# Edge counting in 29 spans of unequal widths, formed one span ahead

## The chip, the cores and the metric

One Trainium2 chip, one core of it. The metric is the device time of one execution in microseconds; lower is better. The core's engines work in parallel, each on its own list of instructions: PE (TensorE) multiplies matrices into PSUM, DVE (VectorE) and ACT (ScalarE) do elementwise work, POOL (GpSimd) gathers rows, SP (SyncE) starts transfers. They wait for one another by semaphores.

## What is computed

A graph transformer of two layers on 1250 nodes with 768 features and 20,000 edges `(src, dst)`, sorted by `dst`. The first layer adds an edge attention (12 heads), a linear attention without softmax (`mix`) and a mixture of experts; the second a graph convolution, another mixer and another mixture of experts. What matters here is the part of the first layer that needs the edges:

```
dst = minimum(int(1250 * uniform(20000) ** 2), 9999);  order = argsort(dst)
xn  = layernorm(x)
e   = leaky_relu(a1[src] + a2[dst]);  w = exp(e - segment_max(e, dst)[dst])
agg = segment_sum(w / denom[dst] * ft[src], dst)       # the edge attention
q, k, v = elu(xn @ w_qkv) + 1 ...;  out = (q (k^T v)) / (q sum(k)) @ w_proj
x   = x + relu(agg + res) + out
```

Edges are not evenly spread: `dst` is the square of a uniform number, so the number of edges that end below node n is about 20000 * sqrt(n / 1250). The first 50 nodes receive some 4,000 edges, the last 50 some 400.

## The kernel before

**Counting.** The kernel turns the edge list into a dense matrix `AT[s, d]`, the number of edges from s to d, and does the attention on it. It counts by matmuls of one-hot rows. The edges lie in 160 tiles of 125 edges. A node `src` is written as (row `src mod 125`, block `src div 125`). For a span of `WD` = 50 destination nodes, DVE forms for each tile that holds edges of the span two one-hot matrices: `OHS` (125 edges x 128 rows, from `io128`) and `OHK` (125 edges x 500 columns, from `iok`, column = 10 * (dst - first node) + block). PE multiplies the two and accumulates in a PSUM bank: 125 x 500 counts. ACT copies the bank into `AT` (`counts_out`). There are `NW` = 25 spans of 50 nodes.

**Turns.** A span's tiles are worked in turns of `SLOTS` = 3 tiles, in a hardware loop on DVE (`hot_rows`) and one on PE (`span_counted`). How many turns a span has is worked out on the chip from the edges (a table that both engines load) and is at least 2. The formed matrices go through a ring of `RING` = 4 turns, so DVE can be at most four turns ahead of PE. The counts alternate between two PSUM banks (`WB` = 2), which leaves six banks for the other work.

**Where the counting stands.** Spans 0 to 12 (`QSPANS`, `WQ` = 13) are counted between the 18 rounds in which PE computes the queries of the linear attention (L830, six q blocks times three column chunks): after rounds 1 to 13 PE counts one span each. In each round ACT takes an exponential of the result (L1243, L1245), DVE combines it into `QT` (L1756). DVE forms span r - 1 ahead of its emptying of round r. I call this the query stage. Spans 13 to 24 are counted in the tile stage, ten node tiles t of 125 nodes: for each PE transposes the attention rows of tile t (L856), makes the rows of tile t + 2 (`linear`, L847), counts the first span of `TILE_SPANS[t]`, multiplies by the projection for tile t - 1 in two halves (L864), with the tile's second span, if any, between the halves. DVE does in tile t: `normal_rows(t + 2)` (L1764, L1768), the forming of the tile's second span, the addition of one projection half (`add_half`, L1776), the forming of the *first* span of tile t + 1, and the other addition. Before `linear(0)`, PE waits until DVE has emptied all 18 query rounds. SP loads the projection's weights once 13 spans have left PSUM.

Behind the tile stage comes the edge attention proper, which needs the whole of `AT`; then the mixtures of experts and the second layer, which don't depend on the counting otherwise.

With the inputs of this case the turns of the 25 spans are 11, 5, 4, 3, 3, 3, 3, 3 and then 2 each: 45 in the query stage and 24 in the tile stage, 69 in all.

Of the kernel before, what the change touches and what calls it, by code (L numbers as in the profile page):

```python
# [32 lines left out]
CH = [(0, 418), (418, 416), (834, 416)]  # L33
# [20 lines left out]
WSLOTS = 6  # L54
QSPANS = {r: r - 1 for r in range(1, 14)}
WQ = len(QSPANS)
TILE_SPANS = [[WQ + t + (t > 3) + (t > 6)] + ([WQ + t + (t > 3) + 1] if t in (3, 6) else []) for t in range(NT)]
assert [w for t in TILE_SPANS for w in t] == list(range(WQ, NW))
FILLS = [(p, t0, nt) for p in range(NP) for t0, nt in ((0, 4), (4, 4), (8, 2))]
FILL_AT = {1: 0, 4: 1, 6: 2}  # L60
DEN_AT = {3: (1, 3), 7: (5, 7), 9: (9,)}
# [99 lines left out]
def graph_transformer(nc, xn_d, y_d, x, src, dst, gW, gWT, gWresT, attnT, w0, wp0, bp0, rwT, rb, ewT, eb,  # L161
                      W1, b1c, W2, b2, w1, wp1, bp1, fgT, fbg, fW1, fb1, fW2, fb2, out):
    J = plan_jobs()


    cursor = [(nc.sbuf_base + 63) // 32 * 32]
# [118 lines left out]
    vv = sb("vv", [P, 2 * H])  # L285
    iok = sb("iok", [T, KW], F16)
    gidx = sb("gidx", [80, 2, NW])
    gidx_i = sb("gidx_i", [80, 2, NW], I32)
    tidx = sb("tidx", [80, 2])
    tidx_i = sb("tidx_i", [80, 2], I32)  # L290
    mnx = sb("mnx", [80, 2, 2])
    hit = sb("hit", [80, 2, 2, NW])
    rng = sb("rng", [2 * NW, 1])
    span = sb("span", [1, 8, NW])
    table = sb("table", [1, 3, NW], I32)
    assert cursor[0] <= top - XNB * C * 4 - 8192
# [288 lines left out]
    def _(pool):  # L585
# [6 lines left out]
        nc.gpsimd.iota(k128_i, pattern=[[P, 32]], base=0, channel_multiplier=0).then_inc(consts, 1)  # L592
        nc.gpsimd.iota(tq_i, pattern=[[1, NT]], base=0, channel_multiplier=0).then_inc(consts, 1)
        nc.gpsimd.iota(io128_i, pattern=[[1, P]], base=0, channel_multiplier=0).then_inc(consts, 1)
        nc.gpsimd.iota(gidx_i, pattern=[[WD, 2], [WD, NW]], base=0, channel_multiplier=0).then_inc(consts, 1)
        nc.gpsimd.iota(tidx_i, pattern=[[80, 2]], base=0, channel_multiplier=1).then_inc(consts, 1)
        nc.gpsimd.iota(iok_i, pattern=[[1, KW]], base=0, channel_multiplier=0).then_inc(consts, 1)

# [96 lines left out]
    def _(pe):  # L695
# [104 lines left out]
            emptied(J.last_in(8 - WB + b, J.at["q0_0"]))  # L800

        def span_counted(w):
            ps = PS[:, 8 - WB + w % WB, 0:KW]
            OHS, OHK = (OHSA, OHKA) if w < WQ else (OHSB, OHKB)

            def counted(first):
                formed = nc.tensor.snap(formed_r, min_val=0, max_val=2 * SLOTS * TURNS * NW)
                ring = nc.tensor.snap(ring_r, min_val=0, max_val=RING - 1)
                for k in range(SLOTS):
                    pe.wait_ge(oh_ready, formed + 2 * k + 2)  # L810
                    nc.tensor.matmul(ps, OHS[:, bass.ds(ring, 1), k, :].rearrange("p a c -> p (a c)"),  # L811
                                     OHK[:, bass.ds(ring, 1), k, :].rearrange("p a c -> p (a c)"),
                                     start=(first and k == 0), stop=True, skip_group_check=True).then_inc(oh_free, 1)
                nc.tensor.reg_alu(formed_r, formed_r, 2 * SLOTS, ALU.add)
                nc.tensor.reg_alu(ring_r, ring_r, 1, ALU.add)
                nc.tensor.reg_alu(ring_r, ring_r, RING - 1, ALU.bitwise_and)

            if w >= WB:
                pe.wait_ge(at_ready, w - WB + 1)
            counted(True)  # L820
            with nc.tensor.Fori(1, turns_of[w]):
                counted(False)
            nc.tensor.matmul(ps[:, 0:16], zeros, zeros[:, 0:16], start=False, stop=True,
                             skip_group_check=True).then_inc(acc_done, 1)

        for q in range(KC):
# [8 lines left out]
            if q == 1:  # L835
# [2 lines left out]
                for k in range(NT):  # L838
                    last = nc.tensor.transpose(ps[0:T, k * H:(k + 1) * H], ARW[0:H, k * T:(k + 1) * T], ident[0:H, 0:H])
                last.then_inc(pe_filled, 1)  # L840
        pe.wait_ge(dve_emptied, J.emptied("dve", J.at[f"q0_{KC - 1}"] + 2))

        def linear(t):
            for b in range(2):
                ps = begin(J.at[f"lin{t}"] + b)
                for p in range(3):
                    last = nc.tensor.matmul(ps[0:T, p * (P + 2):(p + 1) * (P + 2)], QT[:, 3 * b + p, t * T:(t + 1) * T],  # L847
                                            KVB[:, 3 * b + p, :], start=True, stop=True)
                last.then_inc(pe_filled, 1)
# [377 lines left out]
    def _(act):  # L1227
# [38 lines left out]
        def counts_out(w):  # L1266

            act.wait_ge(acc_done, w + 1)
            nc.scalar.activation(AT[:, :, w * WD:(w + 1) * WD], PS[0:T, 8 - WB + w % WB, 0:KW].rearrange("p (d s) -> p s d", s=NT),
                                 ACT.Copy).then_inc(at_ready, 1)  # L1270

        for r in range(18):
# [251 lines left out]
    def _(dve):  # L1524
# [75 lines left out]
        for t in range(NT):  # L1600
# [126 lines left out]
        def hot_rows(w):  # L1727

            OHS, OHK = (OHSA, OHKA) if w < WQ else (OHSB, OHKB)
            nc.vector.reg_alu(tile_r, window[w], TBITS - 1, ALU.bitwise_and)  # L1730
            nc.vector.reg_alu(end_r, window[w], (1 << 20) - TBITS, ALU.bitwise_and)
            with nc.vector.Fori(0, nc.vector.snap(end_r, min_val=2 * TBITS, max_val=TURNS * TBITS), TBITS):
                done = nc.vector.snap(done_r, min_val=0, max_val=SLOTS * TURNS * NW)
                ring = nc.vector.snap(ring_r, min_val=0, max_val=RING - 1)
                tile = nc.s_assert_within(nc.vector.snap(tile_r, min_val=0, max_val=TBITS - 1), 0, ETP - SLOTS,
                                          skip_runtime_bounds_check_because=
                                          "a window's first tile is at most ETP less the tiles of its turns")
                for k in range(SLOTS):
                    dve.wait_ge(oh_free, done + k + 1)
                    V.tensor_scalar(OHS[:, bass.ds(ring, 1), k, :].rearrange("p a c -> p (a c)"), io128,  # L1740
                                    ES[:, 0, bass.ds(tile + k, 1)], None, ALU.is_equal).then_inc(oh_ready, 1)
                    V.tensor_scalar(OHK[:, bass.ds(ring, 1), k, :].rearrange("p a c -> p (a c)"), iok,
                                    ES[:, 1, bass.ds(tile + k, 1)], -float(KW * w), ALU.subtract,
                                    ALU.is_equal).then_inc(oh_ready, 1)
                nc.vector.reg_alu(tile_r, tile_r, SLOTS, ALU.add)
                nc.vector.reg_alu(done_r, done_r, SLOTS, ALU.add)
                nc.vector.reg_alu(ring_r, ring_r, 1, ALU.add)
                nc.vector.reg_alu(ring_r, ring_r, RING - 1, ALU.bitwise_and)

        for r in range(18):  # L1750
            o, n = CH[r % 3]
            if r in QSPANS:
                hot_rows(QSPANS[r])
            ps = full(J.at[f"q0_{r // 3}"] + r % 3)
            dve.wait_ge(qexp, r + 1)
            V.scalar_tensor_tensor(out=QT[:, r // 3, o:o + n], in0=ps[:, 0:n], scalar=0.0, in1=TQ[r % 4 // 2][:, r % 2, 0:n],  # L1756
                                   op0=ALU.max, op1=ALU.add).then_inc(dve_emptied, 1)
# [446 lines left out]
```

## Time and profile before

| | us |
|---|---|
| time, median of 3 runs | 1899.55 (1899.08 to 1900.85) |
| profiled execution, its own time | 1895.67 |
| its span in the profile | 1893.9 |
| mean granted TensorE clock, share of full | 0.969 |
| PE busy | 1774.6 (94%) |
| DVE busy | 723.1 (38%) |
| ACT busy | 391.8 (21%) |

The span runs from the first to the last instruction of the profiled execution; a few microseconds of its time lie around it. Engines overlap, so the busy times don't add up to the span. "PEld" is PE's loading of the stationary operand, which lies beside its multiplying; "PEldq" and "DVEq" rows are an engine's sequencer at work on registers and branches. In a timeline each row is a start, a length, an engine, a line of the kernel, an operation with output and input, and a count of merged instructions; in brackets stands the idle time of the engine before it and who released it.

### The profile page before, as it was taken

What the parts mean: (1) busy time and instruction counts of PE and PEld (TensorE: products, weight loads), DVE (VectorE), ACT (ScalarE), POOL (GpSimd) and SP (SyncE); (2) the same over time, 40 slices, a digit from 0 to 9 for tenths busy, and PEclk for the clock granted to TensorE, in tenths of its full rate; (3) what the DMA queues carried; (4) which work ended last, traced back from release to release, by engine and by line L of the source; (5) the groups of instructions that cost most, each with busy time, mean ns of one, the idle gap of its engine ahead of it and who ended that gap; (6) DMA issues with size and microseconds to landing.
All of it is one profiled execution on the core that took longest, in us unless ns stands there. A gap on an engine that the chain in (4) does not pass through costs nothing.

```text
span 1893.9 us, 24577 instructions
## 1 busy us (share of the span) xinstructions
PE 1774.6 (94%) x7984; PEld 1088.4 (57%) x7985; DVE 723.1 (38%) x1799; ACT 391.8 (21%) x1030; POOL 130.3 (7%) x170
## 2 busy tenths in 40 slices
PE   7999899999999986899997999999999999789996
PEld 4555455664333343566666855555579569656664
DVE  4321674555789897211116211151111114522221
ACT  2441022112422222110113321000221221112221
POOL 0000000000000000111114000000000000012222
PEclk9999799999999998899998999999999999889999
DMA  6002101000001014355636011010010012535773
GB/s 195 1 0 71 57 2 61 1 1 33 26 28 49 28 39 149 134 189 180 211 132 189 29 50 50 0 50 0 0 51 1 0 58 87 219 78 148 203 189 60
DMA packets 53660, 144.38 MB, mean 76 GB/s; under 512 B 9806, under 2 KB 20450, under 8 KB 53125
## 3 DMA queue, kind: packets, MB, share of 16 engines
q1 hardware_dynamic: 34053, 87.05, 13.3%
q0 software_dynamic: 12032, 36.23, 7.9%
q10 hardware_dynamic: 7488, 19.93, 3.0%
q8 instruction: 55, 0.90, 0.2%
q14 instruction: 32, 0.26, 0.0%
HBM read 114.08 MB, written 33.99 MB: 78 GB/s over the span
## 4 chain that ended last, share of the span: by engine, by line
PE 84%; DVE 8%; DMA 2%; issue 2%; DVEq 2%; ACT 1%; ACTq 0%; POOL 0%; SPq 0%; POOLq 0%
PE PS L723 21%; PE PS L1064 10%; PE PS L733 8%; PE PS L1174 5%; PE PS L1196 5%; PE PS L830 4%; PE PS L864 4%; PE PS L1146 4%; PE PS L1132 4%; PE PS L1105 4%; DVE WRA L1849 3%; PE PS L970 3%; PE PS L811 3%; PE PS L1042 2%; PE PS L979 2%
## 5 line engine op out<-in xcount | busy, mean ns | idle before, releaser
L723 PE MATMUL PS<-WS,XT 128*125 128x384 f32 x960 | 312.9, 488 | 1.4 <-issue 1.4
L723 PEld LDWEIGHTS PS<-WS,XT 128*125 128x125 f32 x960 | 180.2, 189 | 129.1 <-issue 3.0
L1064 PE MATMUL PS<-WS,XGT 128*128 x600 | 199.3, 489 | 0.0
L1064 PEld LDWEIGHTS PS<-WS,XGT 128*128 128x128 f32 x600 | 113.0, 192 | 74.4 <-issue 1.9
L733 PE MATMUL PS<-XT,WS 128*128 128x416 f32 (+1 forms) x432 | 151.2, 512 | 0.0
L1849 DVE SCALAR_TENSOR_TENSOR WRA<-RB,U,AT 125x500 f32<-125x500 f32 (+1 forms) x240 | 140.0, 647 | 2.5 <-issue 0.6
L1983 DVE TENSOR_TENSOR YS<-PS,EBB 128x768 f32<-128x768 f32 x48 | 46.0, 958 | 243.9 <-PE PS L1064 191.1
L733 PEld LDWEIGHTS PS<-XT,WS 128*128 128x128 f32 x432 | 81.6, 189 | 69.2 <-issue 69.2
L970 PE MATMUL PS<-WRA,F 125*64 125x500 f32 (+1 forms) x480 | 100.0, 527 | 10.2 <-DVE WRA L1849 9.1
L614 POOL DMA_INDIRECT XG<-xn_rows,IDX x53 | 52.1, 982 | 749.1 <-DVEq L1944 641.7
L1174 PE MATMUL PS<-WS,XGT 128*128 x288 | 99.7, 497 | 1.1 <-ACTq L1393 1.1
L1196 PE MATMUL PS<-WS,HT 128*128 x276 | 92.9, 486 | 1.1 <-DVE YS L1983 1.1
L1391 ACT ACTIVATE XGT<-PS 128x384 f32<-128x384 f32 x102 | 44.5, 488 | 227.4 <-DVE YS L1983 176.2
L830 PE MATMUL PS<-XT,WS 128*128 128x416 f32 (+1 forms) x216 | 83.4, 540 | 0.3 <-DVEq L1714 0.3
L864 PE MATMUL PS<-WS,QT 128*125 128x384 f32 x240 | 80.2, 490 | 0.0
L1105 PE MATMUL PS<-XT,WS 128*128 128x250 f32 x360 | 78.3, 378 | 0.6 <-issue 0.6
L1468 ACT ACTIVATE HF<-PS,DT 125x384 f32<-125x384 f32 x40 | 23.2, 581 | 263.0 <-PE PS L723 263.0
L723 PE MATMUL PS<-WS,QK 128*125 128x384 f32 x240 | 77.6, 486 | 0.0
L2070 DVE TENSOR_TENSOR HH<-HF,HH 125x384 fp32r<-125x384 f32 x40 | 22.3, 558 | 136.5 <-ACT HH L1470 136.5
L1174 PEld LDWEIGHTS PS<-WS,XGT 128*128 128x128 f32 x288 | 54.1, 195 | 34.9 <-issue 4.2
L1196 PEld LDWEIGHTS PS<-WS,HT 128*128 128x128 f32 x276 | 52.4, 190 | 37.6 <-issue 1.3
L1105 PEld LDWEIGHTS PS<-XT,WS 128*128 128x128 f32 x360 | 68.7, 192 | 9.1 <-issue 1.0
(314 smaller groups left out, 2105.0 us busy)
## 6 DMA issues: line engine op xcount, KB each, us to landing
WS<-in_ewT SPq DMA_DIRECT2D x8, 2304.0 KB, 10.6
WS<-in_fW SPq DMA_DIRECT2D x16, 1152.0 KB, 6.9
WS<-in_w SPq DMA_DIRECT2D x5, 2304.0 KB, 10.4
expert_rows<-YS ACTq DMA_DIRECT2D x25, 384.0 KB, 2.3
xn_rows<-XN ACTq DMA_DIRECT2D x20, 336.0 KB
RB<-expert_rows SPq DMA_DIRECT2D x12, 488.3 KB
WS<-in_wp SPq DMA_DIRECT2D x2, 2304.0 KB, 8.4
WS<-in_W SPq DMA_DIRECT2D x2, 2304.0 KB, 8.4
```

Of the source, the lines that this page charges most:

```text
L723: last = nc.tensor.matmul(ps[0:T, 0:HC], lhsT[:, k, t * T:(t + 1) * T], w[:, k, b * HC:(b + 1) * HC], start=(k == 0), stop=(k == KC - 1))
L733: last = nc.tensor.matmul(ps[:, 0:n], w[:, k, q * P:(q + 1) * P], rhs[:, k, o:o + n], start=(k == 0), stop=(k == KC - 1))
L830: last = nc.tensor.matmul(ps[:, 0:n], w[:, k, q * P:(q + 1) * P], XT[:, k, o:o + n], start=(k == 0), stop=(k == KC - 1))
L864: last = nc.tensor.matmul(ps[0:T, 0:HC], QT[:, k, t * T:(t + 1) * T], w[:, k, b * HC:(b + 1) * HC], start=(k == 0), stop=(k == KC - 1))
L970: last = nc.tensor.matmul(num[j * D:(j + 1) * D], F[:, s, 2 * p + j, 0:D], WR[k % WSLOTS][:, j, 0:n], start=(s == 0), stop=(s == NT - 1), ...
L1064: last = nc.tensor.matmul(PS[:, 4 + 2 * a + b, 0:HC], XGT[:, a, k, :], WS[:, bass.ds(slot, 1), k * C + b * HC:k * C + (b + 1) * HC].rearra ...
L1105: last = nc.tensor.matmul(ps[:, 0:n], w[:, k, q * P:(q + 1) * P], XT[:, k, o:o + n], start=(k == 0), stop=(k == KC - 1))
L1132: last = nc.tensor.matmul(ps[:, 0:n], HH[:, v, s, q * P:(q + 1) * P], AT[:, s, o:o + n], start=(s + v == 0), stop=(s == NT - 1 and v == 1))
L1146: last = nc.tensor.matmul(ps[0:T, 0:HC], AT[:, s, t * T:(t + 1) * T], HH[:, v, s, b * HC:(b + 1) * HC], start=(s + v == 0), stop=(s == NT ...
L1174: last = nc.tensor.matmul(PS[:, 2 + a, 0:FH], XGT[:, a, k, :], WS[:, bass.ds(slot, 1), k * FH:(k + 1) * FH].rearrange("p a b -> p (a b)"), ...
L1196: last = nc.tensor.matmul(PS[:, 5 + b, 0:HC], HT[:, k, :], WS[:, bass.ds(slot, 1), o:o + HC].rearrange("p a b -> p (a b)"), start=(k == 0) ...
L1849: V.scalar_tensor_tensor(out=WR[k % WSLOTS][:, j, 0:nt * T], in0=RBS[u % RSLOTS][:, j, 0:nt * T], scalar=U[:, s, h:h + 1], in1=AT[:, s, t0 ...
```

## The change

The destination nodes are cut into 29 spans. 21 are 50 nodes wide and go downward from the last node to node 200 (`START` = 1200, 1150, ... 200); eight more start at 153, 112, 78, 50, 28, 12, 3 and 0, with widths 47, 41, 34, 28, 22, 16, 9 and 3. The compare for `OHK`, the matmul and the copy to `AT` run over the span's own width (`kw` = 10 x width columns) instead of 500. The query stage counts the first 13 spans in the new order (nodes 1200 down to 600), the tile stage the other 16: one, then two in tiles 1 to 6, then one in tiles 7 to 9. DVE forms span 0 ahead of the query rounds, and span r ahead of its emptying of round r, one span earlier than before. PE's wait before `linear` is for the column chunk that tile t needs. The spans' limits, by which the table of turns is made, are written by 16 more small memsets on DVE.

```diff
-NW = N // WD
+WIDE = 21
+NARROW = [153, 112, 78, 50, 28, 12, 3, 0]
+NW = WIDE + len(NARROW)
+START = [N - WD * (w + 1) for w in range(WIDE)] + NARROW
+WIDTH = [WD] * WIDE + [a - b for a, b in zip([START[WIDE - 1]] + NARROW, NARROW)]
...
-TILE_SPANS = [[WQ + t + (t > 3) + (t > 6)] + ([WQ + t + (t > 3) + 1] if t in (3, 6) else []) for t in range(NT)]
+NSPANS = [1, 2, 2, 2, 2, 2, 2, 1, 1, 1]
+TILE_SPANS = [list(range(WQ + sum(NSPANS[:t]), WQ + sum(NSPANS[:t + 1]))) for t in range(NT)]
...
         def span_counted(w):
-            ps = PS[:, 8 - WB + w % WB, 0:KW]
+            kw = WIDTH[w] * NT
+            ps = PS[:, 8 - WB + w % WB, 0:kw]
...
-                                     OHK[:, bass.ds(ring, 1), k, :].rearrange("p a c -> p (a c)"),
+                                     OHK[:, bass.ds(ring, 1), k, 0:kw].rearrange("p a c -> p (a c)"),
...
-        pe.wait_ge(dve_emptied, J.emptied("dve", J.at[f"q0_{KC - 1}"] + 2))
-
         def linear(t):
+            c = next(c for c, (o, n) in enumerate(CH) if (t + 1) * T <= o + n)
+            pe.wait_ge(dve_emptied, J.emptied("dve", J.at[f"q0_{KC - 1}"] + c))
...
         def counts_out(w):
...
-            nc.scalar.activation(AT[:, :, w * WD:(w + 1) * WD], PS[0:T, 8 - WB + w % WB, 0:KW].rearrange("p (d s) -> p s d", s=NT),
+            nc.scalar.activation(AT[:, :, START[w]:START[w] + WIDTH[w]],
+                                 PS[0:T, 8 - WB + w % WB, 0:WIDTH[w] * NT].rearrange("p (d s) -> p s d", s=NT),
...
             if t == 0:
+                for w in range(WIDE, NW):
+                    V.memset(gidx[:, 0, w:w + 1], float(START[w]))
+                    V.memset(gidx[:, 1, w:w + 1], float(START[w] + WIDTH[w]))
                 dve.wait_ge(e_in, 32)
                 V.tensor_copy(EF, EI).then_inc(edge_f, 1)
...
-                    V.tensor_scalar(OHK[:, bass.ds(ring, 1), k, :].rearrange("p a c -> p (a c)"), iok,
-                                    ES[:, 1, bass.ds(tile + k, 1)], -float(KW * w), ALU.subtract,
+                    V.tensor_scalar(OHK[:, bass.ds(ring, 1), k, 0:kw].rearrange("p a c -> p (a c)"), iok[:, 0:kw],
+                                    ES[:, 1, bass.ds(tile + k, 1)], -float(NT * START[w]), ALU.subtract,
                                     ALU.is_equal).then_inc(oh_ready, 1)
...
+        hot_rows(0)
         for r in range(18):
             o, n = CH[r % 3]
-            if r in QSPANS:
-                hot_rows(QSPANS[r])
+            if r in QSPANS and QSPANS[r] + 1 < WQ:
+                hot_rows(QSPANS[r] + 1)
```

The first place is DVE at the start of the query stage. `OHSA` and `OHKA` are the one-hot buffers of the spans of this stage, `QT<-PS,TQ` is the emptying of a query round, `L1732` and `L1745` the loop over a span's turns. Before, around the emptyings of rounds 0 and 1:

```order
L1721 MEMSET zeros 125x64
L1756 SCALAR_TENSOR_TENSOR QT<-PS,TQ_104 128x418
...
L1740 TENSOR_SCALAR OHSA<-io_66,ES 125x128
L1742 ISA
L1742 TENSOR_SCALAR OHKA<-iok,ES 125x500
...
L1732 COMPARE_AND_BRANCH
L1756 SCALAR_TENSOR_TENSOR QT<-PS,TQ_104 128x416
```

And in the changed kernel:

```order
L1733 MEMSET zeros 125x64
...
L1753 TENSOR_SCALAR OHSA<-io_66,ES 125x128
L1755 ISA
L1755 TENSOR_SCALAR OHKA<-iok,ES 125x500
...
L1745 COMPARE_AND_BRANCH
L1770 SCALAR_TENSOR_TENSOR QT<-PS,TQ_104 128x418
...
L1745 COMPARE_AND_BRANCH
L1770 SCALAR_TENSOR_TENSOR QT<-PS,TQ_104 128x416
```

A loop of forming now stands ahead of the emptying of round 0 as well; the emptying of round 1 has the loop of span 1 ahead of it and no longer that of span 0.

The second place is PE in the tile stage, from the first projection half of one tile to the counting of the next; `OHKB` and `OHSB` are the one-hot buffers of this stage, `L823` and `L831` close a span. Before, at a tile with one span:

```order
L823 MATMUL PS<-zeros 128x16
L864 MATMUL PS<-WS,QT 125x384 x12
L856 MATMUL PS<-ident,LO 128x125 x6
L847 MATMUL PS<-KVB,QT 125x130 x6
...
L811 MATMUL PS<-OHKB,OHSB 128x500
```

In the changed kernel, at the end of tile 4 and the start of tile 5:

```order
L872 MATMUL PS<-WS,QT 125x384 x6
...
L819 MATMUL PS<-OHKB,OHSB 128x470
...
L831 MATMUL PS<-zeros 128x16
L872 MATMUL PS<-WS,QT 125x384 x6
L864 MATMUL PS<-ident,LO 128x125 x6
L855 MATMUL PS<-KVB,QT 125x130 x6
...
L819 MATMUL PS<-OHKB,OHSB 128x410
```

The projection of a tile, 12 matmuls in a row before, is now cut in two by a span in tiles 1 to 6, and the counting matmuls have the span's own width.

## Rows read from the trace of the kernel before

**Rows 1.** Chain of work that ended last, shares of the span by engine

```profile
PE 84%; DVE 8%; DMA 2%; issue 2%; DVEq 2%; ACT 1%; ACTq 0%; POOL 0%; SPq 0%; POOLq 0%
```

**Rows 2.** Windows: us, busy us of each engine, granted clock, DMA share, GB/s

```profile
197.00:330.00 133.00, 125.40 (x419) 62.04 (x419) 78.64 (x307) 29.57 (x54) 0.00 (x0) 0.92 0.07 23
220.00:229.00 9.00, 7.95 (x17) 2.64 (x17) 7.14 (x31) 0.59 (x1) 0.00 (x0) 0.50 0.00 0
330.00:445.00 115.00, 113.56 (x476) 70.70 (x476) 54.77 (x190) 15.47 (x33) 0.00 (x0) 0.99 0.00 1
332.00:336.00 4.00, 3.94 (x21) 3.81 (x21) 2.57 (x10) 1.56 (x3) 0.00 (x0) 0.57 0.00 0
```

**Rows 3.** Timeline of PE in the query stage

```profile
197.19 11.25 PE L830 MATMUL PS<-XT,WS 128*128 128x418 f32 x24 [0.26 <-DVEq L1714]
208.28 1.73 PE L811 MATMUL PS<-OHKA,OHSA 125*128 x6
...
226.22 6.19 PE L830 MATMUL PS<-XT,WS 128*128 128x416 f32 x12
...
255.81 1.25 PE L839 MATMUL PS<-ident,ARW 12*125 12x12 f32 x10
...
281.26 4.44 PE L830 MATMUL PS<-XT,WS 128*128 128x416 f32 x12
...
286.83 4.44 PE L830 MATMUL PS<-XT,WS 128*128 128x416 f32 x12
...
303.57 17.03 PE L830 MATMUL PS<-XT,WS 128*128 128x416 f32 x48
```

**Rows 4.** Timeline of DVE while it forms span 0: starts of two turns

```profile
222.42 0.26 DVE L1740 TENSOR_SCALAR OHSA<-io,ES 125x128 bf16 x1 [0.43 <-PE PS L811]
...
222.85 0.25 DVE L1740 TENSOR_SCALAR OHSA<-io,ES 125x128 bf16 x1
...
224.21 0.26 DVE L1740 TENSOR_SCALAR OHSA<-io,ES 125x128 bf16 x1 [0.43 <-PE PS L811]
```

**Rows 5.** Timeline of all engines, first node tile

```profile
29.62 0.41 DVE L1614 CAST EF<-EI 80x500 f32<-80x500 int32 x1
...
32.22 0.56 PE L756 MATMUL PS<-ident,EF 80*125 80x80 f32 x4
```

**Rows 6.** Timeline of PE in the tile stage

```profile
322.52 2.94 PE L847 MATMUL PS<-KVB,QT 128*125 128x130 f32 x24 [1.92 <-DVE QT L1756]
...
329.08 1.23 PE L811 MATMUL PS<-OHKB,OHSB 125*128 x3 [1.40 <-DVE OHSB L1740]
...
345.88 0.81 PE L856 MATMUL PS<-ident,LO 125*128 125x125 f32 x6
...
347.86 1.43 PE L811 MATMUL PS<-OHKB,OHSB 125*128 x6
...
349.16 7.99 PE L864 MATMUL PS<-WS,QT 128*125 128x384 f32 x24
```

**Rows 7.** Line L811 (counting matmuls), sequencer row: ns min/median/max

```profile
L811 PEldq FUSED_REGOPS  x207: 74/74/93, 206.8 to 425.2; - x104
```

**Rows 8.** Timeline of DVE in the tile stage

```profile
331.58 0.20 DVE L1764 RECIPROCAL LD<-PS 125x6 f32<-125x6 f32 x1
...
334.14 0.25 DVE L1740 TENSOR_SCALAR OHSB<-io,ES 125x128 bf16 x1 [0.76 <-issue]
...
335.97 0.26 DVE L1740 TENSOR_SCALAR OHSB<-io,ES 125x128 bf16 x1 [0.46 <-issue]
...
337.35 0.20 DVE L1764 RECIPROCAL LD<-PS 125x6 f32<-125x6 f32 x1
...
353.95 0.26 DVE L1740 TENSOR_SCALAR OHSB<-io,ES 125x128 bf16 x1
...
356.29 0.25 DVE L1740 TENSOR_SCALAR OHSB<-io,ES 125x128 bf16 x1 [0.60 <-issue]
...
444.45 0.56 DVE L1776 TENSOR_TENSOR X<-PS,X 125x384 f32<-125x384 f32 x1 [5.06 <-PE PS L864]
```

More of the change, by code:

```diff
@@ L45 @@
 WD = 50
-NW = N // WD
+WIDE = 21
[3 more added lines that the diff above has]
+WIDTH = [WD] * WIDE + [a - b for a, b in zip([START[WIDE - 1]] + NARROW, NARROW)]
+assert sum(WIDTH) == N and max(WIDTH) == WD
 KW = WD * NT
@@ L56 @@
 WQ = len(QSPANS)
-TILE_SPANS = [[WQ + t + (t > 3) + (t > 6)] + ([WQ + t + (t > 3) + 1] if t in (3, 6) else []) for t in range(NT)]
-assert [w for t in TILE_SPANS for w in t] == list(range(WQ, NW))
+NSPANS = [1, 2, 2, 2, 2, 2, 2, 1, 1, 1]
+TILE_SPANS = [list(range(WQ + sum(NSPANS[:t]), WQ + sum(NSPANS[:t + 1]))) for t in range(NT)]
+assert WQ + sum(NSPANS) == NW
 FILLS = [(p, t0, nt) for p in range(NP) for t0, nt in ((0, 4), (4, 4), (8, 2))]
@@ L287, in graph_transformer @@
     gidx = sb("gidx", [80, 2, NW])
-    gidx_i = sb("gidx_i", [80, 2, NW], I32)
     tidx = sb("tidx", [80, 2])
@@ L293, in graph_transformer @@
     rng = sb("rng", [2 * NW, 1])
+    gidx_i = sb("gidx_i", [80, 2, NW], I32)
+    cursor[0] -= (2 * NW * 4 + 31) // 32 * 32
     span = sb("span", [1, 8, NW])
@@ L594, in _ @@
         nc.gpsimd.iota(io128_i, pattern=[[1, P]], base=0, channel_multiplier=0).then_inc(consts, 1)
-        nc.gpsimd.iota(gidx_i, pattern=[[WD, 2], [WD, NW]], base=0, channel_multiplier=0).then_inc(consts, 1)
+        nc.gpsimd.iota(gidx_i, pattern=[[WD, 2], [-WD, NW]], base=START[0], channel_multiplier=0).then_inc(consts, 1)
         nc.gpsimd.iota(tidx_i, pattern=[[80, 2]], base=0, channel_multiplier=1).then_inc(consts, 1)
@@ L1729, in hot_rows @@
             OHS, OHK = (OHSA, OHKA) if w < WQ else (OHSB, OHKB)
+            kw = WIDTH[w] * NT
             nc.vector.reg_alu(tile_r, window[w], TBITS - 1, ALU.bitwise_and)
```

## Prediction, made before the changed kernel was run

> **What bounds the kernel now.** I read the chain of work that ended last first: PE holds 84% of it [rows 1]. Then I cut out the two stretches that the change touches. The query stage and the tile stage together are 248 us, and PE is busy for 125.4 of 133 us and for 113.6 of 115 us [rows 2]. So a microsecond is won only where PE has less to multiply, waits less, or runs at a higher clock. The reader is to see both losses in the query stage. At 208.28 PE begins to count span 0 and at 226.22 it goes on with the next query round: 17.9 us [rows 3] for 33 matmuls. It is DVE that sets this pace: from one turn's first compare to the next it takes 1.79 us (222.42 to 224.21) [rows 4], while PE needs 0.64 us for a turn (below). PE is shown as nearly busy there only because its clock was granted at half, 1.2 GHz, from 220 to 229 [rows 2]; the next round still pays for it.
>
> Prices that I use, all at the full clock. A query round with one span of two turns: 281.26 to 286.83, 5.58 us [rows 3]. Such a span alone, six matmuls and the closing one: 347.86 to 349.16, 1.30 us [rows 6], so 0.64 us a turn and 0.03 for the close; a query round alone 4.28. Transposes and `linear` of a tile: 345.88 to 347.86, 1.98 us; two projection halves: 349.16 to about 357.0 (the last row's 7.99 less its overlap of about 0.17), 3.92 each [rows 6].
>
> **How many turns.** From the sorted `dst` list of this case I counted which tiles of 125 edges each new span touches, three to a turn. The 17 spans from node 1200 down to 400 have 2 turns, the next nine (nodes 350 to 28) 3, span [12, 28) 4, the last two 3: 71 turns against 69. What matters is where they lie: 26 instead of 45 in the query stage, 45 instead of 24 in the tile stage.
>
> **Query stage.** PE's first 24 matmuls stay as they are (11.1 us, 197.19 to 208.28). Then span 0 costs 1.3 us instead of 17.9, twelve rounds of 5.58 are 67.0, the small transposes of L839 1.3, and the last four rounds 17.0 [rows 3]. Sum 97.7 us. Before it was 197.19 to 320.6, 123.4 us. Gain **25.7 us**: 16.6 on span 0, 1.7 on the round after it at half clock (6.03 against 4.3), the rest on spans 1 to 7, which had 3 to 5 turns. Does DVE keep up? Its share of a round is two turns, 3.21 us (334.14 to 337.35) [rows 8], and about 0.65 for the emptying, which I take as long as an addition of the tile stage (below): 3.9 of 5.58. It also forms one span ahead, and two spans are four turns, just what the ring holds. So no wait of PE is left here.
>
> **Start of the kernel.** 16 memsets of about 0.1 us stand ahead of the cast of the edges. The cast is at 29.62 and PE takes it up at 32.22 [rows 5]: 1.6 us into a gap of 2.2. Nothing. If the cover were gone they would cost 1.6 us. Four more table loads on PE and DVE go beside matmuls. Nothing.
>
> **Tile stage, the work of PE.** Before: 12 spans of 2 turns, 15.6 us. After: four wide spans of 2 turns (5.2), four wide ones of 3 turns (7.8), and eight narrow ones. For these I need the price of a turn with fewer columns. The columns alone would give 0.6 us for 470, 0.28 for 220, 0.04 for 30. But PE's sequencer has work in each turn that doesn't shrink: three register operations of 74 ns [rows 7] and the loop's own. The lower bound is the columns, the upper one the 0.64 of a wide turn, which shows no gap. I take 0.5 us where the columns need less. The narrow spans then cost 1.8, 1.6, three times 1.5, 2.0 and twice 1.5: 13.0. Sum 26.0, **10.5 us more** (8.3 by the columns with 0.1 us a matmul, 13.3 if narrow turns cost 0.64).
>
> **Tile stage, the waits.** DVE's work in a tile with two 3-turn spans is 2.56 for `normal_rows` up to the first compare (331.58 to 334.14), twice 5.0 for the forming (3.21 and one turn of 1.83 more, 334.14 to 335.97), and twice 0.64 for the additions of 0.56 [rows 8]: 13.9 us. PE's in the same tile is 1.98 + 2 x 1.94 + 7.84 = 13.7. So DVE becomes as loaded as PE in tiles 3 and 4, and is a little below it later. A narrower compare saves DVE (500 - kw) x 0.26 ns, since 0.43 us a pair [rows 4] is only partly columns. I walked both queues tile by tile with these durations, 0.17 us for a handover from DVE to PE and the ring's limit. Times are from the end of the last query matmul. For the kernel before, the walk ends at 122.7 where the trace has 123.7 (320.6 to the last projection half, which DVE takes up at 444.45 [rows 8]). For the changed kernel the tiles end at 10.2, 25.7, 39.1, 53.0, 66.8, 80.1, 93.0, 104.8, 114.8, 124.8, and the stage at 134.4: **11.7 us more**. That is 10.5 of work, 2.1 of new waits (0.6 in tile 1, about 0.3 in each of tiles 2 to 6, where the third turn of the second span is formed just as PE gets to it) and 0.9 less at the entry. There the wait of 1.92 us before `linear` [rows 6] goes, but what PE does earlier soon waits for DVE again: PE waited 1.40 us at 329.08 for the first compares, these follow two `normal_rows`, and DVE can begin those only 0.9 us earlier, once query round 17 is emptied.
>
> The Trainium skill (VectorE: DVE Perf Modes, The TRN2 errata) speaks against narrow spans: VectorE pays a fixed cost for each instruction, about 150 cycles measured, whatever the width. The trace agrees in kind. By that figure a compare of 30 columns takes 0.16 us against 0.14 by my slope, an estimate of 1.3 us over the 66 compares of the narrow spans behind node 112, and the sum would be some tenths less favourable.
>
> **Bounds of the waits.** If DVE were never last, the stage would be 7.4 to 8.2 us longer than before. If a turn cost DVE 0.35 us more, as the one from 353.95 to 356.29 did (2.34 us) [rows 8], the walk gives +18.4.
>
> **Sum.** -25.7 + 11.7 = -14.0 us, against the profiled execution's own 1895.67 (span 1893.9): 1881.7. The median of the runs shown is 3.9 us above that execution, so I state 1899.55 - 14.0 = **1885.5 us**. The bounds give -18.3 and -7.3: 1881 to 1892. Everything behind the tile stage only starts earlier.
>
> **The rivals.**
>
> *Nothing waits, and narrow turns cost their columns.* PE pulls its sequencer's work ahead while it does the projection. For it: the wide turns show no gap. Against: a narrow turn gives less cover than its register work. -25.7 + 7.4 = -18.3, 1881 us.
>
> *The tile stage loses the clock.* At the entry PE had waited twice, and from 332 to 336 its granted clock was 0.57 [rows 2]. The query round after span 0 shows what such a stretch costs: 1.7 us. If the new waits bring this in each of tiles 1 to 6, it is 10 us: 1896 us; in half of them 1891. Against: the waits are 0.3 us each among 13 us of work. The Trainium skill (TensorE: Matmul & The Clock Gate, HAM oscillation) says the same in kind: gaps in PE's work drop its clock; the trace agrees at 220 us and at 332 us.
>
> *The forming isn't ahead, and it is slower than before.* If PE had to wait for the whole forming of the second span in tiles 1 to 6, that would be 5.0 us each, 30 us in all, and the sum +14: 1914 us. It decides as soon as PE waits 2.3 us more than in my walk in each of the six tiles. The ring is for it: two 3-turn spans are six turns and the ring holds four. Against: PE does 3.9 us of projection between the two spans, and DVE fills the ring in that time.
>
> *The gain is given back.* Later stages wait for transfers in places, so an earlier start could be lost there. Against: none of their loads has a fixed time, all are issued by what the chain does. Within 0.2% of no change.
>
> **Chances.** My forecast with its own range of 1882 to 1889: 0.6. Nothing waits: 0.17. The clock, in whole or in part: 0.13. Given back: 0.05. Slower: 0.05. About 0.2% is what a measurement of this kernel can tell from no change, 3.8 us. A small part of the clock case falls within it. Faster 0.91, same 0.05, slower 0.04. The range reaches over the first rival and over half of the clock case: 1879 to 1893 us.
>
> **What the profile of the changed kernel would show.** Right: the query stage about 98 us long, the closing matmul of span 0 about 1.3 us after its start, every round with a span 5.6 us apart, the clock at full there; no DVE release of a counting matmul in that stage. The tile stage about 134 us from the last query matmul, with short waits of L819 for DVE's one-hot buffers in tiles 1 to 6, and turns of 0.5 us in the last tiles. Wrong: a tile that takes 15 us or more, a granted clock below 0.9 in the tile stage, a turn of the 30-column span above 0.64 us on PE, or stages behind it that are longer than before.

## The result, and the profile after

The changed kernel takes 1889.59 us (median of 5 runs, 1887.73 to 1892.89), the kernel before 1899.55: 10.0 us less. The ratio is 0.9945, 95% interval 0.9931 to 0.9959. Run once more, beside the experiments, the changed kernel had 1891.97 us and a ratio of 0.9958 (0.9942 to 0.9974). It is faster, by half a per cent. The forecast of 1885.5 was 4 us too low: the time lies 0.6 us above the 1882 to 1889 that I gave my own forecast, and within the whole range of 1879 to 1893.

Timeline of PE in the changed kernel, from the first query round to the last span of the tile stage (start, length, engine, line, operation, count; in brackets the idle time and who ended it):

```profile
197.26 10.60 PE L838 MATMUL PS<-XT,WS 128*128 128x418 f32 x24 [0.25 <-DVEq L1726]
207.70 1.44 PE L819 MATMUL PS<-OHKA,OHSA 125*128 x6
208.97 0.17 PE L831 MATMUL PS<-zeros 125*128 125x16 bf16 x1
209.00 4.44 PE L838 MATMUL PS<-XT,WS 128*128 128x416 f32 x12
213.27 1.44 PE L819 MATMUL PS<-OHKA,OHSA 125*128 x6
...
214.57 4.46 PE L838 MATMUL PS<-XT,WS 128*128 128x418 f32 x12
...
294.12 2.83 PE L855 MATMUL PS<-KVB,QT 128*125 128x130 f32 x24
...
301.56 1.23 PE L819 MATMUL PS<-OHKB,OHSB 125*128 x3 [1.39 <-DVE OHSB L1753]
...
391.54 0.58 PE L819 MATMUL PS<-OHKB,OHSB 125*128 x6
392.31 0.73 PE L819 MATMUL PS<-OHKB,OHSB 125*128 x3 [0.19 <-DVE OHKB L1755]
393.62 0.77 PE L819 MATMUL PS<-OHKB,OHSB 125*128 x3 [0.58 <-issue]
...
394.74 7.98 PE L872 MATMUL PS<-WS,QT 128*125 128x384 f32 x24
...
403.19 0.73 PE L819 MATMUL PS<-OHKB,OHSB 125*128 x7
404.13 0.21 PE L819 MATMUL PS<-OHKB,OHSB 125*128 x1 [0.21 <-DVE OHKB L1755]
404.55 0.21 PE L819 MATMUL PS<-OHKB,OHSB 125*128 x1 [0.21 <-DVE OHKB L1755]
...
413.58 0.30 PE L819 MATMUL PS<-OHKB,OHSB 125*128 x6
```

Against [rows 3]: span 0 is counted in 1.3 us (207.70 to 209.00) where it took 17.9, and a round with a span takes 5.57 (209.00 to 214.57). The query stage is 96.9 us long, 197.26 to 294.1, against 123.2. Against [rows 6]: `linear` starts at 294.12 without a wait. The tile stage then takes 138.7 us, up to 432.85, against 123.9. The balance at the end of the last projection half is 444.3 - 432.85 = 11.5 us.

The windows of the changed kernel (us, busy us of PE, PEld, DVE, ACT, POOL, granted clock, DMA share, GB/s):

```profile
197.00:294.00 97.00, 96.75 (x318) 50.81 (x318) 48.04 (x179) 27.42 (x50) 0.00 (x0) 0.98 0.08 26
294.00:433.00 139.00, 131.48 (x588) 80.58 (x586) 85.96 (x331) 17.68 (x39) 0.00 (x0) 0.99 0.01 4
205.00:230.00 25.00, 25.00 (x85) 12.79 (x84) 16.55 (x65) 6.63 (x12) 0.00 (x0) 1.00 0.00 1
303.00:307.00 4.00, 3.60 (x15) 2.63 (x16) 2.93 (x11) 1.56 (x3) 0.00 (x0) 0.58 0.02 4
```

The reader is to see three things against [rows 2]. In the query stage PE is busy for 96.75 of 97 us. From 205 to 230, where the kernel before ran at half clock for 9 us and more, the clock is now full. And in the tile stage PE is busy for 131.5 of 139 us, so it has 7.5 us of gaps. Before it had 4.3 in the same stage (119.5 us busy of 123.8, from 320.5 to 444.3); the 1.4 of 115 us in [rows 2] leave out the entry. What PE waited for in this stage (us in all, times, longest), first in the kernel before, then in the changed one:

```profile
PE PS L811 <- DVE OHSB L1740: 2.0, 2, 1.4
PE PS L847 <- DVE QT L1756: 1.9, 1, 1.9
```

```profile
PE PS L819 <- DVE OHSB L1753: 2.5, 3, 1.4
PE PS L819 <- DVE OHKB L1755: 1.6, 8, 0.2
PE PS L831 <- issue: 0.9, 4, 0.3
PE PS L864 <- DVEq L1785: 0.9, 2, 0.5
PE PS L819 <- issue: 0.6, 1, 0.6
```

Behind the tile stage the profile of the changed kernel is 3.4 us *longer* than that of before (1453.0 against 1449.6 us). The code there is the same. In its second profile it is 1457.5 us, with 97.2 us in the query stage and 138.7 again in the tile stage (I had expected 96.9 and 138.7 within 0.6, and a time of 1888 to 1893). So what the later stages take varies by some 5 us between executions of one kernel. The stretches at a lower clock stand at the same places in both profiles and differ in depth: the granted clock is 0.71 in the first and 0.63 in the second from 734 to 780 us, and 0.66 in both from 980 to 1010.

### The profile page after: what moved, and what is told of

Read it like the earlier page. It is cut to its first block, busy times and chain, and to the rows that moved or that the text cites. A ratio compares the mean times of both kernels' runs of the same rounds, so it can differ in the third digit from the quotient of the medians.

```text
span 1885.8 us, 24720 instructions
## 1 busy us (share of the span) xinstructions
PE 1766.0 (94%) x7994; PEld 1089.7 (58%) x7995; DVE 724.2 (38%) x1827; ACT 392.3 (21%) x1034; POOL 131.8 (7%) x170
## 3 DMA queue, kind: packets, MB, share of 16 engines
q1 hardware_dynamic: 34053, 87.05, 13.3%
## 4 chain that ended last, share of the span: by engine, by line
PE 85%; DVE 8%; issue 2%; DVEq 2%; DMA 2%; ACT 1%; ACTq 0%; POOL 0%; SPq 0%; POOLq 0%
PE PS L730 21%; PE PS L1072 10%; PE PS L740 8%; PE PS L1182 5%; PE PS L1204 5%; PE PS L838 4%; PE PS L1113 4%; PE PS L872 4%; PE PS L1154 4%; PE PS L1140 4%; DVE WRA L1863 3%; PE PS L978 3%; PE PS L819 2%; PE PS L1050 2%; PE PS L987 2%
## 5 line engine op out<-in xcount | busy, mean ns | idle before, releaser
L1182 PEld LDWEIGHTS PS<-WS,XGT 128*128 128x128 f32 x288 | 54.1, 195 | 34.7 <-issue 3.7
```

What stands on the lines that cost most here:

```text
L1182: last = nc.tensor.matmul(PS[:, 2 + a, 0:FH], XGT[:, a, k, :], WS[:, bass.ds(slot, 1), k * FH:(k + 1) * FH].rearrange("p a b -> p (a b)"), ...
```

## The experiments

The two stages are short enough to read a cause from one profile, where the total is not. The table gives, for each run, the time and ratio, the query stage (first to last query matmul) and the tile stage (from there to the end of the last projection half), both from PE's timeline, and what lies behind.

| run | median us | ratio (95%) | query | tile | behind |
|---|---|---|---|---|---|
| kernel before, profile | 1899.55 | 1 | 123.2 | 123.9 | 1449.6 |
| changed kernel | 1889.59 | 0.9945 (0.9931 to 0.9959) | 96.9 | 138.7 | 1453.0 |
| changed, again | 1891.97 | 0.9958 (0.9942 to 0.9974) | 97.2 | 138.7 | 1457.5 |
| DVE at 500 columns | 1892.61 | 0.9949 (0.9931 to 0.9967) | 97.9 | 139.1 | 1456.7 |
| DVE and PE at 500 columns | 1890.70 | 0.9945 (0.9927 to 0.9964) | 97.5 | 139.2 | 1456.3 |
| not formed ahead | 1891.42 | 0.9951 (0.9936 to 0.9967) | 97.5 | 140.5 | 1454.6 |
| old wait before `linear` | 1894.25 | 0.9965 (0.9948 to 0.9982) | 97.9 | 141.6 | 1455.0 |
| only formed ahead | 1896.02 | 0.9986 (0.9973 to 0.9998) | 118.6 | 124.3 | 1453.0 |
| equal spans, descending | 1899.90 | 0.9999 (0.9988 to 1.0009) | 97.1 | 151.4 | 1453.9 |
| a drain in each turn | 1911.68 | 1.0063 (1.0045 to 1.0082) | 97.3 | 161.2 | 1455.4 |
| ascending order | 1884.30 | 0.9908 (0.9888 to 0.9928) | 100.8 | 128.7 | 1456.0 |
| ascending, again | 1884.57 | 0.9928 (0.9914 to 0.9943) | 101.3 | 128.7 | 1453.6 |
| ascending, with the drain | 1897.37 | 0.9986 (0.9976 to 0.9995) | 109.8 | 131.8 | 1454.5 |
| mixed order | 1888.38 | 0.9942 (0.9927 to 0.9957) | 100.6 | 132.9 | 1454.0 |

**Do narrow columns earn anything?** First DVE alone at full width, then PE too.

```diff
         def hot_rows(w):
...
-            kw = WIDTH[w] * NT
+            kw = KW
```

> The changed kernel, but DVE compares all 500 columns of every span, also of the narrow ones; PE still multiplies only the span's own width. Theory (a pair of compares on DVE has a fixed spacing of 0.42 us whatever the width, so narrow spans save DVE nothing): the tile stage stays at 138.7 us from the last query matmul to the last projection half, within 0.5 us, and the time within 2 us of the changed kernel's 1889.6. Rival (my prediction's slope of 0.26 ns a column): the tile stage grows by 2 to 3 us.

The tile stage was 139.1 us, 0.3 longer. For the stage the theory holds and my slope falls. The time, 1892.61, is 3.0 us above 1889.6 and so outside the 2 us that I gave: the query stage was 1.0 us and what lies behind 3.7 us longer, where the edit changes nothing on PE. The second run makes the same edit in `span_counted`.

> The changed kernel, with both DVE's compares and PE's counting matmuls at 500 columns for every span. Theory (PE's narrow turn costs its columns, but DVE sets the pace of the tile stage): the counting matmuls of the tile stage cost 5 to 6 us more, of which 2 to 4 us show in the stage, since PE waits for DVE less. Rival (PE's sequencer sets a floor of 0.5 us a turn, as predicted): at most 3 us more work and less than 2 us in the stage.

The tile stage was 139.2 us: 0.5 longer, where the theory had 2 to 4. The rival's numbers hold, less than 2 us in the stage. PE's timeline of this kernel shows why, in the last three tiles:

```profile
390.80 0.81 PE L864 MATMUL PS<-ident,LO 125*128 125x125 f32 x6
...
392.78 3.00 PE L819 MATMUL PS<-OHKB,OHSB 125*128 x12
...
403.78 0.81 PE L864 MATMUL PS<-ident,LO 125*128 125x125 f32 x6
404.43 2.07 PE L819 MATMUL PS<-OHKB,OHSB 125*128 x9
...
414.32 0.81 PE L864 MATMUL PS<-ident,LO 125*128 125x125 f32 x6
```

The tiles still follow each other at 13.0 us (390.80 to 403.78) and 10.5 (403.78 to 414.32). In the changed kernel it is 13.0 and 10.4. PE counts nine matmuls of 500 columns without a gap in 1.9 us; with 90 columns it does seven in 0.73 us and waits for the last two, with 30 six in 0.30 and waits for the last three. In tiles 8 and 9 PE's work at 500 columns fills the time in which it would else wait for DVE.

Tile 7, with the span of 4 turns, is another case. From the first counting matmul to the projection its span takes 3.19 us at 500 columns (392.78 to 395.97) and 3.20 at 160 in the changed kernel (391.54 to 394.74). There DVE's last compare ends at 392.27, 1.35 us before PE starts the last turn. The first spans of tiles 5 and 6 don't wait for DVE either: their last compares end at 363.10 and 376.77, and PE comes at 364.16 and 377.91. Each takes 1.77 us, at 410 and at 280 columns, and 1.94 at 500. So a turn of three matmuls keeps a price on PE that hardly falls with the columns. What sets it, these runs don't show.

**Is forming ahead needed?** The changed kernel with `hot_rows(w)` in round w + 1 again.

```diff
-        hot_rows(0)
         for r in range(18):
             o, n = CH[r % 3]
-            if r in QSPANS and QSPANS[r] + 1 < WQ:
-                hot_rows(QSPANS[r] + 1)
+            if r in QSPANS:
+                hot_rows(QSPANS[r])
```

> The changed kernel, with each span formed behind the emptying of the round before, as in the kernel before. Theory (a round has room for two turns either way, the gain of the query stage is all in the turns): only span 0 waits for DVE, 1 to 2 us, the rest of the rounds stay at 5.58 us, the time is 1 to 3 us above the changed kernel. Rival (forming ahead is what keeps PE from waiting): each of 13 rounds is longer than 5.6 us, 5 us or more in all.

The query stage was 97.5 us, 0.7 longer (0.3 to 0.7 against the two profiles of the changed kernel). The theory is right in kind and its 1 to 2 us for span 0 is too high. The time is not told apart from the changed kernel's. The tile stage was 1.8 us longer, nearly all in tile 7: see the wait before `linear` below. The other half of the question is the kernel before with this edit reversed, and nothing else:

> The kernel before with DVE forming one span ahead, and nothing else of the change. Theory: the wait at the first compare goes, but DVE still sets the pace of the 11 turns of span 0, which begins 2 to 6 us earlier: 3 to 7 us less in the query stage, 1893 to 1898 us. Rival (forming ahead carries the gain): 10 us or more less.

4.6 us less in the query stage, ratio 0.9986. As the theory has it: PE counted six turns at once and reached the end of span 0 at 221.6 instead of 226.2, and then still took DVE's pace of 1.79 us a turn.

**Is it the order or the cut?** 25 equal spans, in the new order.

```diff
-WIDE = 21
-NARROW = [153, 112, 78, 50, 28, 12, 3, 0]
+WIDE = 25
+NARROW = []
...
-NSPANS = [1, 2, 2, 2, 2, 2, 2, 1, 1, 1]
+NSPANS = [1, 1, 1, 2, 1, 1, 2, 1, 1, 1]
```

> The old cut, 25 spans of 50 nodes, in the new descending order and formed ahead; the spans of 3, 4, 5 and 11 turns come in the tile stage. It takes the narrow spans out of the change and leaves the order. Theory (the gain needs both, since the 11 turns of the first 50 nodes wait for DVE wherever they stand): query stage 97 us, tile stage 146 to 151 us, near 1900 us, within 5 us of the kernel before. Rival (the order alone is the gain): 1893 us or less.

Query stage 97.1, tile stage 151.4, ratio 0.9999. The order, with the forming ahead, moves the loss to the tile stage, where the first 50 nodes' 11 turns stand last; the gain needs the cut. The tile stage lies 0.4 us above the range that I gave.

**Does DVE's forming set the pace of the tile stage?** One more drain a turn, which costs DVE time and PE nothing.

```diff
                                     ALU.is_equal).then_inc(oh_ready, 1)
+                V.drain()
                 nc.vector.reg_alu(tile_r, tile_r, SLOTS, ALU.add)
```

> The changed kernel with one drain more on DVE at the end of each turn of forming, so that a turn takes DVE 0.1 to 0.3 us longer than 1.79 and PE's work stays. Theory (DVE's turns set the pace of the tile stage and have room in the query stage): the query stage stays at 97 us within 0.7, the tile stage grows by 35 to 45 times the longer turn, so 4 to 12 us. Rival (PE's work sets both stages): less than 2 us in the tile stage.

DVE's timeline of this kernel, two turns of the 90-column span:

```profile
416.70 0.26 DVE L1753 TENSOR_SCALAR OHSB<-io,ES 125x128 bf16 x1
...
418.81 0.25 DVE L1753 TENSOR_SCALAR OHSB<-io,ES 125x128 bf16 x1 [0.84 <-issue]
```

A turn takes 2.11 us instead of 1.79. The query stage stays at 97.3, the tile stage grows by 22.4 us to 161.2. The theory is right on where, and too low on how much: 45 turns x 0.32 is 14. The windows show where the rest comes from:

```profile
197.00:294.00 97.00, 96.87 (x316) 50.78 (x317) 47.52 (x177) 27.41 (x50) 0.00 (x0) 0.97 0.08 26
370.00:446.00 76.00, 67.91 (x263) 40.18 (x262) 36.79 (x147) 6.79 (x17) 0.00 (x0) 0.89 0.00 1
```

From 370 to 446 the granted clock is 0.89, where it was 1.00 in the changed kernel from 320 on. Five rows of the projection are each 1.6 to 1.7 us longer than in the changed kernel, two of them here:

```profile
383.05 5.68 PE L872 MATMUL PS<-WS,QT 128*125 128x384 f32 x12
...
410.34 9.56 PE L872 MATMUL PS<-WS,QT 128*125 128x384 f32 x24
```

They took 4.11 and 7.98 at the full clock. Together the five make 8.2 us, and the 14.2 that are left are what the longer turns come to. Tile 7 grew by the clock alone: its span of 4 turns took 3.18 us, as in the changed kernel. PE's waits of about 1 us for DVE in tiles 4, 5 and 6 are new, but the one in tile 4 has no such stretch behind it, so that the waits bring the half clock is argued from this one run. The reversed order takes the same drain:

> The ascending order with the same drain. Theory (its tile stage has room on DVE, 2 + 2 turns a tile, its query stage has none, 3 turns a round): the query stage grows by 3 to 9 us from 100.8, the tile stage stays at 128.7 within 2 us. Rival: the same growth as in the changed kernel, in the tile stage.

Here the query stage grew by 8.9 us to 109.8 and the tile stage by 3.1 to 131.8. So each order is sensitive where it has 3 turns to a round or 3 + 3 to a tile. The 3.1 is 1.1 more than expected; 2.3 of it is in tile 1 (17.75 us instead of 15.42), behind the waits at the entry.

**Ascending order.** The narrow and 3-turn spans go to the query stage (39 turns), the 16 last, of 2 turns each, to the tile stage (32).

```diff
-START = [N - WD * (w + 1) for w in range(WIDE)] + NARROW
-WIDTH = [WD] * WIDE + [a - b for a, b in zip([START[WIDE - 1]] + NARROW, NARROW)]
+START = NARROW[::-1] + [N - WD * (WIDE - w) for w in range(WIDE)]
+WIDTH = [b - a for a, b in zip(START, START[1:] + [N])]
...
-        nc.gpsimd.iota(gidx_i, pattern=[[WD, 2], [-WD, NW]], base=START[0], channel_multiplier=0).then_inc(consts, 1)
+        nc.gpsimd.iota(gidx_i, pattern=[[WD, 2], [WD, NW]], base=N - WD * NW, channel_multiplier=0).then_inc(consts, 1)
...
-                for w in range(WIDE, NW):
+                for w in range(len(NARROW)):
```

> The same 29 spans in ascending order: the eight narrow ones and the four wide ones of 3 turns come in the query stage (39 turns), the tile stage has 16 spans of 2 turns (32 turns). Theory (DVE's forming sets the pace of the changed kernel's tile stage at 3 + 3 turns a tile): PE waits less there, the tile stage falls from 138.7 to 128 to 131 us; the query stage, where DVE now has 5.7 us of work a round, grows from 96.9 to 100 to 103 us. The sum is 3 to 6 us below the changed kernel. Rival (the tile stage's length is PE's work and handovers, not DVE's turns): the tile stage falls by less than 3 us and the time does not fall.

Both stages came as the theory has them, 100.8 and 128.7 us, together 6.1 us less. PE's timeline, the transposes that open tiles 4 to 6:

```profile
348.79 0.81 PE L864 MATMUL PS<-ident,LO 125*128 125x125 f32 x6
...
361.26 0.81 PE L864 MATMUL PS<-ident,LO 125*128 125x125 f32 x6
...
373.75 0.81 PE L864 MATMUL PS<-ident,LO 125*128 125x125 f32 x6
```

A tile with two spans takes 12.5 us, each of them, where the changed kernel has 13.7 to 14.5. By PE's work it is 1.98 + 2 x 1.30 + 7.84 = 12.4. Nothing waits there any more. But PE also counts 13 turns fewer in this stage, so not all of the 10 us are waits for DVE that went. In the query stage narrow spans whose matrices were formed ahead were cheap on PE, first of all the one of 30 columns, nine matmuls from 207.41 to 207.66:

```profile
207.41 0.38 PE L819 MATMUL PS<-OHKA,OHSA 125*128 x9
...
207.66 4.44 PE L838 MATMUL PS<-XT,WS 128*128 128x416 f32 x12
```

The repeat:

> The ascending order once more on this chip: query stage 100.8 us and tile stage 128.7 us within 0.5 each; its time 1882 to 1887 us, 5 to 7 us below the changed kernel's.

1884.57 us, stages of 101.3 and 128.7. The interval of the first run of this order, 0.9888 to 0.9928, lies below both intervals of the changed kernel; that of the repeat, 0.9914 to 0.9943, overlaps the first of them and just touches the second. By the stages, which repeat to 0.5 us in both kernels, the order is 5.6 to 6.5 us ahead. It is the fastest of the kernels run here. A mixed order was to balance both stages further:

```diff
+START = [1200, 350, 1150, 300, 153, 1100, 250, 112, 200, 1050, 78, 50, 28] + list(range(1000, 399, -50)) + [12, 3, 0]
+WIDTH = [min([s for s in START + [N] if s > a]) - a for a in START]
```

> The same 29 spans in a mixed order: nine of 3 turns and four of 2 in the query stage (35 turns), one or two of 2 turns in tiles 0 to 6, the three narrowest alone in tiles 7 to 9. The limits are all written by memsets early, where DVE waits for the input. Theory (a stage is as long as the slower of DVE's turns and PE's work, tile by tile): query stage 98 to 101 us, tile stage 128 to 131 us, 1 to 3 us below the ascending order, so 1881 to 1884. Rival (what counts is only that no tile has 3 + 3 turns): the same as the ascending order within 1 us.

The query stage came as expected (100.6), the tile stage (132.9) and the time (1888.38) did not, and the rival's time doesn't fit either. Tiles 2 to 6 take 12.5 us as in the ascending order, but tiles 7 and 8, with the 160- and 90-column spans of 4 and 3 turns, take 13.0 and 10.4 instead of 11.1 and 9.8, and tile 1 16.0 instead of 15.4. In tile 9 the span of 30 columns and 3 turns takes 2.3 us, where the ascending order has one of 2 turns and 1.3 us. In tiles 8 and 9 PE's last matmuls wait for DVE: a single span is formed between the two projection halves' additions, so DVE has little more than 4 us before PE wants it, room for 2 turns and not for 3. In tile 7, which loses most, it is not DVE. Its last compare for that span, and PE's rows:

```profile
389.34 0.26 DVE L1755 TENSOR_SCALAR OHKB<-iok,ES 125x160 f16 x1
```

```profile
389.35 1.49 PE L819 MATMUL PS<-OHKB,OHSB 125*128 x9
391.43 0.73 PE L819 MATMUL PS<-OHKB,OHSB 125*128 x3 [0.58 <-issue]
...
392.54 7.98 PE L872 MATMUL PS<-WS,QT 128*125 128x384 f32 x24
```

All matrices are there at 389.60, and PE still starts the last turn 1.8 us later. The span takes 3.19 us, up to 392.54. That is the 3.2 us of the changed kernel, of the run at 500 columns and of the run with the drain: a price of PE's own for four turns, whatever the columns and DVE's pace.

**The wait before `linear`.** The changed kernel with the old wait for all 18 rounds.

```diff
-            c = next(c for c, (o, n) in enumerate(CH) if (t + 1) * T <= o + n)
-            pe.wait_ge(dve_emptied, J.emptied("dve", J.at[f"q0_{KC - 1}"] + c))
```

> The changed kernel with the old wait ahead of the linear rows: PE waits until DVE has emptied all 18 query rounds. Theory: PE waits 1.9 us at that place again, but only about 0.9 us of it shows in the tile stage, 139.6 instead of 138.7. Rival: all 1.9 us show, 140.6.

The tile stage was 141.6 us, more than either. PE's timeline shows both parts of it:

```profile
298.08 2.94 PE L855 MATMUL PS<-KVB,QT 128*125 128x130 f32 x24 [1.92 <-DVE QT L1770]
300.86 0.81 PE L864 MATMUL PS<-ident,LO 125*128 125x125 f32 x6
...
304.31 1.23 PE L819 MATMUL PS<-OHKB,OHSB 125*128 x3 [1.31 <-DVE OHSB L1753]
```

```profile
397.74 9.67 PE L872 MATMUL PS<-WS,QT 128*125 128x384 f32 x24
407.24 0.81 PE L864 MATMUL PS<-ident,LO 125*128 125x125 f32 x6
```

The entry: the last query matmul ends at 296.0, PE waits 1.92 us, and the first counting matmul stands 8.3 us behind it (304.31), against 7.4 in the changed kernel (294.1 to 301.56). That is the 0.9 of the theory. The other 2 us are in tile 7: its 24 projection matmuls take 9.5 us (397.74 to 407.24) where they take 7.8 at full clock. The granted clock is 0.83 from 395 to 405, right behind the 4-turn span with its short gaps. The same tile is 14.7 instead of 13.0 us in the kernel that doesn't form ahead, where the clock is 0.83 too. In the two profiles of the changed kernel it is 13.0, at a clock of 1.00, with nearly the same gaps in the span (0.58 us ahead of the last turn, against 0.66 and 0.62). Whether the edit brings it or chance, these runs don't tell.

## Why the prediction was right, and by how much it was off

**What bounds, and the query stage: right.** Predicted 97.7 us and a gain of 25.7; measured 96.9 and 26.4. Span 0 at 1.3 us, the rounds at 5.57, no wait of a counting matmul for DVE, the clock full. The first 24 matmuls took 10.4 us instead of the 11.1 that I carried over; over the fourteen profiles the same matmuls took 9.9 to 11.5, so the 0.7 us by which this stage beat the forecast are within chance.

**The start of the kernel: right.** The first query matmul stands at 197.26, before at 197.19.

**The turns: right**, 26 and 45; the trace has 78 and 135 counting matmuls.

**The tile stage: the term that was mis-sized.** Predicted 11.7 us more, measured 14.9. From the first counting matmul of each span to the next row of other work, PE spent 34.7 us on the stage's spans, against 18.4 before: 16.3 more, where the prediction had 10.5 of work and 2.1 of waits. The way from the last query matmul to the first counting matmul is 1.2 us shorter (7.4 against 8.6), where I had 0.9. The eight narrow spans alone took 17.4 us, where I had 13.0 and some 0.9 of waits. So nearly all that is missing is there, and two steps of the prediction put it too low: DVE's pace and PE's price of a narrow turn.

**DVE's pace: wrong.** The sentence is "A narrower compare saves DVE (500 - kw) x 0.26 ns". DVE's timeline of the changed kernel, in the span of 160 columns and in that of 30:

```profile
385.62 0.25 DVE L1753 TENSOR_SCALAR OHSB<-io,ES 125x128 bf16 x1
385.79 0.26 DVE L1755 TENSOR_SCALAR OHKB<-iok,ES 125x160 f16 x1
386.05 0.26 DVE L1753 TENSOR_SCALAR OHSB<-io,ES 125x128 bf16 x1
...
387.42 0.26 DVE L1753 TENSOR_SCALAR OHSB<-io,ES 125x128 bf16 x1 [0.52 <-issue]
```

```profile
409.92 0.25 DVE L1753 TENSOR_SCALAR OHSB<-io,ES 125x128 bf16 x1
410.08 0.24 DVE L1755 TENSOR_SCALAR OHKB<-iok,ES 125x30 f16 x1
410.34 0.25 DVE L1753 TENSOR_SCALAR OHSB<-io,ES 125x128 bf16 x1
...
411.71 0.25 DVE L1753 TENSOR_SCALAR OHSB<-io,ES 125x128 bf16 x1 [0.54 <-issue]
```

The compare itself is shorter, 0.26 and 0.24 us against 0.35, but the next pair starts 0.42 us after the one before at either width, and the next turn 1.80 and 1.79 us after, as in [rows 4]. I had read a duration's slope as a saving of pace. The full-width run shows the same from the other side. Where DVE's compares come last this costs time: tiles 8 and 9 took 10.4 us each, where my walk has 10.0. In tile 4 it had 13.8 and the trace has 14.5; the second span there, of 470 columns, takes 2.66 us, and 2.66 at 500 columns too, and its last compare ends only 0.6 us before the closing matmul (357.50 and 358.11).

**The price of a narrow turn on PE: too low, and not a fixed one.** I took 0.5 us a turn where the columns need less, and 2.0 us for the span of 4 turns. That span took 3.2 us, 0.8 a turn, in tile 7, which is 13.0 us long where my walk has 11.8; the mixed order shows that it does so with every matrix ready. This is the largest single piece of what is missing, 1.2 us. The first spans of tiles 5 and 6, which didn't wait for DVE, took 1.77 us each where I had 1.6 and 1.5. The other way, PE counted seven matmuls of 90 columns in 0.73 us and six of 30 in 0.30 when it came to a span whose first two turns were ready, and nine of 30 in 0.25 in the ascending order. So the first rival's price, the columns, holds in places, but not for a whole span of 3 or 4 turns in this stage. At 500 columns the stage is only 0.5 us longer. What the unequal widths earn is not fewer columns but fewer turns in one span.

**The Trainium skill's rule** (VectorE: DVE Perf Modes, The TRN2 errata), a fixed cost for each instruction, was cited against narrow spans. The trace agrees in kind, since the compare's duration keeps 0.24 us of its 0.35 when it has 30 columns instead of 500. The estimate from the Trainium skill's figure, 0.16 us, and the 0.14 of my slope are both below that, and below the 0.26 us that lie between the start of that compare and the next.

**The rivals.** *Nothing waits*: refuted, PE has 7.5 us of gaps in the stage, and waits of 4.1 us in it for DVE's one-hot buffers. *The tile stage loses the clock*: in the changed kernel only at the entry, where from 303 to 307 it is 0.58, as before. With the drain, which brings waits of about 1 us, five projection rows had stretches at half clock. Two other runs had one such stretch without longer waits. *Slower*: the drain gives this side too. With 0.32 us more to a turn the kernel is slower than before, ratio 1.0063, though the way there is not the one that this rival names. *Given back*: not shown. The later stages took 1449.6 to 1457.5 us over the fourteen profiles, with no order in it by what was changed; the kernel before has the lowest of these figures, from one profile.

**The signs.** All that I gave for the query stage came. Of those for being wrong, four came too. Tile 1 took 15.4 us, but my own walk has 15.5 for it, so this sign was badly chosen. The clock was below 0.9 at the entry of the tile stage, as before. The last turn of the 30-column span took 1.3 us (414.07 to 415.36), since it waited for DVE: this one did point at the term that failed. The stages behind were 3.4 us longer, within their spread.

**Redone sums.** The two bounds of the tile stage's work, 8.3 and 13.3 us, come to 7.3 and 13.6 from the prices that I gave. The first rival would then be 1880 instead of 1881 us; the measured time is far from both.

**The sum.** The stages gave 11.5 us in the profiles, the medians 10.0. The forecast of 14.0 is off by 3.2 us in the tile stage and by 0.7 the other way in the query stage; what is left, 1.5 us, is within the spread of the later stages.

## What to carry to other kernels

When two engines pass work through a ring, write down for each stretch between two of their meetings what *each* needs there, in time and not in busy share. Then move the pieces until the slower one has room everywhere: here 2 turns between two projection halves cost no wait, and with 3 to most query rounds that stage grew by 3.9 us, PE's own work included. Price a piece on each engine from a row with as many turns: in the tile stage four turns cost PE 0.8 us each, where two cost 0.64. Cutting a piece smaller in columns helps only the engine that is waited for, and only if its pace is set by columns. Read the spacing of starts for this, not the durations.

## What was not expected of the hardware

- The spacing of DVE's compares here is the same at 30, 160 and 500 columns: 0.42 us a pair, 1.79 us a turn of three, though the compare's duration goes from 0.24 to 0.35 us. Each compare has a register operation of 93 ns ahead of it on DVE's sequencer. That this is what sets the spacing is likely, but no run here shows it.
- A drain at the end of a turn costs 0.32 us, and 22 us in a stage of 45 turns: 14.2 by the turns and 8.2 by stretches at half clock.
- PE counted 125-row matmuls of 30 columns at 0.03 to 0.05 us each and of 90 columns at 0.10, each with its own weight load and register operations. But twelve of 160 columns, all ready, took 3.2 us with their closing matmul, no less than twelve of 500, and PE was idle for 0.58 us ahead of the last three. Why, no run here shows.
- Tile 7 was 13.0 us in four runs with this order of spans and 14.7 to 14.9 in two, where a stretch at half clock stands in its projection. What brings it is not shown.
